# Attention and feed-forward block on one core: shift rows issued from ScalarE's queue, the mean of y folded into constants, x normalised in one operation, second query copy ahead of the squares

## The reference

```python
x = x + xattn(layernorm(x), ctx)      # 16 heads, scores of 64 x 64, softmax over the context
x = x + ffn(layernorm(x), w1, w2)     # 256 -> 1024 -> 256

kv_rope = kv_c * cos + rotate_half(kv_c) * sin
scores  = q_r @ k_r.T                  # q_r from Wq, w_kc_q, W_qr; k_r from kv_rope, W_kr
attn    = softmax(scores)
out     = ((attn @ kv_rope) @ w_kc_kv.T) @ Wo.T

def bitlinear158(x, w):
    xn = x / norm(x) * sqrt(d)
    xq = clip(round(xn * s), -128, 127) / s       # s = 127 / max|xn| of the row
    wq = clip(round(w / mean|w|), -1, 1) * mean|w|
    return xq @ wq.T
ffn = bitlinear158(gelu(bitlinear158(x, w1)), w2)
```

## Time and profile before

| | us |
|---|---|
| median of 3 runs | 534.22 |
| the runs | 529.8, 535.0, 534.22 |
| the profiled execution | 530.62, span 528.8 |
| PE busy | 424.0 (80%) |
| DVE busy | 404.1 (76%) |
| ACT busy | 256.1 (48%) |
| POOL busy | 233.6 (44%) |

### The profile page before, as it was taken

One profiled execution on the slowest core, in us unless ns is written; L12 is line 12 of the kernel. 1 busy time (PEld: TensorE's weight loads), 2 busy tenths in 40 slices (PEclk: granted clock), 3 DMA queues, 4 the chain that ended last, 5 costly groups with the idle time before them and its releaser, 6 DMA issues.

```text
span 528.8 us, 9004 instructions
## 1 busy us (share of the span) xinstructions
PE 424.0 (80%) x2823; PEld 298.8 (57%) x2823; DVE 404.1 (76%) x926; ACT 256.1 (48%) x464; POOL 233.6 (44%) x301
## 2 busy tenths in 40 slices
PE   3998787978678788989798989798889877585664
PEld 1488654656546565757485748475647553353432
DVE  0545147888879987989899897988887989886794
ACT  0111263523255646565567474756564747355430
POOL 0300502445334546465555555554645464646432
PEclk9999999999799988999999989998989999987865
DMA  8990901111132303344425253433534344335243
GB/s 237 349 296 1 355 4 43 43 41 43 42 57 61 77 13 93 60 109 74 93 65 104 60 98 62 94 72 81 82 72 76 78 82 73 82 71 114 65 100 80
DMA packets 62800, 48.96 MB, mean 93 GB/s; under 512 B 51169, under 2 KB 56289, under 8 KB 61729
## 3 DMA queue, kind: packets, MB, share of 16 engines
q1 hardware_dynamic: 62752, 48.39, 38.5%
HBM read 32.11 MB, written 4.46 MB: 69 GB/s over the span
## 4 chain that ended last, share of the span: by engine, by line
DVE 30%; DMA 16%; PE 15%; issue 15%; SPq 10%; ACT 3%; POOL 0%; DVEq 0%; ACTq 0%; POOLq 0%
DMA rb<-rinv_d 9%; DMA rinv_d<-ri 5%; DVE cr L841 5%; SPq L422 4%; DVE fw L197 3%; DVE red L811 3%; PE ps L736 3%; DMA shift<-nmax 2%; DVE fw L196 2%; SPq L430 2%; DVE fw L194 2%; DVE red L818 2%; SPq L436 2%; DVE amax L866 2%; DVE ri L834 2%
## 5 line engine op out<-in xcount | busy, mean ns | idle before, releaser
L482 POOL TENSOR_TENSOR cl<-cr,ch 128x512 fp32r<-128x512 f32 x64 | 80.2, 1275 | 178.7 <-ACT ch L563 178.7
L563 ACT ACTIVATE ch<-cr 128x512 fp32r<-128x512 f32 x64 | 39.3, 632 | 100.2 <-DVE cr L841 100.2
L712 PE MATMUL hps<-bh,ch 128*128 128x256 f32 x256 | 78.3, 306 | 8.2 <-issue 8.0
L663 PE MATMUL ps<-xh,ah 128*128 128x256 f32 x256 | 77.5, 303 | 1.7 <-DVE xl L803 1.4
L714 PE MATMUL hps<-bh,cl 128*128 128x256 f32 x256 | 73.8, 288 | 0.0
L713 PE MATMUL hps<-bl,ch 128*128 128x256 f32 x256 | 73.7, 288 | 0.0
L664 PE MATMUL ps<-xl,ah 128*128 128x256 f32 x256 | 72.7, 284 | 0.0
L665 PE MATMUL ps<-xh,al 128*128 128x256 f32 x256 | 72.6, 283 | 0.0
L545 ACT ACTIVATE qf<-ps 128x512 f32<-128x512 f32 x64 | 37.5, 587 | 65.3 <-PE ps L665 65.3
L663 PEld LDWEIGHTS ps<-xh,ah 128*128 128x128 f32 x256 | 49.9, 195 | 19.8 <-issue 16.2
L712 PEld LDWEIGHTS hps<-bh,ch 128*128 128x128 f32 x256 | 51.1, 199 | 11.5 <-issue 11.5
(11 more groups left out here) (116 smaller groups left out, 925.7 us busy)
## 6 DMA issues: line engine op xcount, KB each, us to landing
rb<-rinv_d SPq DMA_DIRECT2D x64, 256.0 KB, 3.9
xs<-x SPq DMA_DIRECT2D x4, 1024.0 KB, 23.1
out<-yo SPq DMA_DIRECT2D x32, 128.0 KB, 2.0
wq_s<-wq SPq DMA_DIRECT2D x1, 2048.0 KB, 20.1
wo_s<-wo_t SPq DMA_DIRECT2D x1, 2048.0 KB, 9.2
w_s<-w_t SPq DMA_DIRECT2D x2, 1024.0 KB, 12.5
rinv_d<-ri SPq DMA_DIRECT2D x128, 2.0 KB, 1.4
wk_a<-wk_t SPq DMA_DIRECT2D x2, 512.0 KB, 6.1
```

The costliest lines, as they stand in the source:

```text
L482: pool.tensor_tensor(cl[:, u % 2, :, b * S:(b + 1) * S], cr[:, :, b * S:(b + 1) * S], ch[:, u % 2, :, b * S:(b + 1) * S].bitcast(F32), ALU ...
L663: pe.matmul(o, ah[:, c, cols], xh[:, k % 2, c, :], start=(c == 0), stop=False)
L712: pe.matmul(O[:, 0:D], c_h, bh[:, hp, :], start=(hp == 0), stop=False)
```

## The change

- `shift_rows` moves from SP's list to ACT's. It stands there behind the first query copy (and `x_hi`) and ahead of `ctx_hi`.
- The mean of y is no longer made on its own. `centre` computes -256 x + sum instead of x - mean, in one operation as before; constants (`least`, `FLOOR1`, the sign of `level`) take up the factor.
- `norm_x` is one operation per tile: x * rstd - mean * rstd, where `nmean` now holds the product.
- The second query copy of a step, `q_out(k, b + 1)`, stands ahead of the squares instead of behind them.
- In PE's list the first `up` of an odd step stands ahead of the shifts instead of behind them.

```diff
@@ -216,10 +214,10 @@
             c = slice(half * NT // 2, (half + 1) * NT // 2)
             n = half * (RSQRT_OPS + 2) + 1
             dve.wait_ge(sem["bn_means"], (half + 1) * NT // 2)
-            dve.tensor_scalar(nmean[:, c], mv[:, c, 0], -1.0, None, ALU.mult).then_inc(sem["rstd_steps"], 1)
             dve.tensor_scalar(nw[0][:, c], mv[:, c, 1], EPS_LN, None, ALU.add).then_inc(sem["rstd_steps"], 1)
-            dve.wait_ge(sem["rstd_steps"], n + 1)
-            rsqrt(dve, nw[0][:, c], rstd[:, c], nw[1][:, c], sem["rstd_steps"], n + 1)
+            dve.wait_ge(sem["rstd_steps"], n)
+            rsqrt(dve, nw[0][:, c], rstd[:, c], nw[1][:, c], sem["rstd_steps"], n)
+            dve.scalar_tensor_tensor(out=nmean[:, c], in0=mv[:, c, 0], scalar=-1.0, in1=rstd[:, c], op0=ALU.mult, op1=ALU.mult).then_inc(sem["rstd_steps"], 1)
 
         cos_t = cst[:, 0:DC]
         em_c = cst[:, 2 * DC:2 * DC + 2 * P]
@@ -258,8 +256,9 @@
             def _(pool):
                 pool.memset(ones[:, :], 1.0).then_inc(sem["const_set"], 1)
                 for k, w in ((0, D), (1, F)):
-                    pool.memset(least[:, 2 * k:2 * k + 2], EPS_N ** 2 * (EPS_LN if k == 0 else 1.0) / w).then_inc(sem["eps_set"], 1)
-                pool.memset(level[:, :], 1.0 / 127.0).then_inc(sem["eps_set"], 1)
+                    pool.memset(least[:, 2 * k:2 * k + 2], EPS_N ** 2 * (EPS_LN * D ** 2 if k == 0 else 1.0) / w).then_inc(sem["eps_set"], 1)
+                pool.memset(level[:, 0:2], -1.0 / 127.0).then_inc(sem["eps_set"], 1)
+                pool.memset(level[:, 2:4], 1.0 / 127.0).then_inc(sem["eps_set"], 1)
                 pool.wait_ge(sem["consts_loaded"], 16)
                 pool.wait_ge(sem["kv_loaded"], 16)
                 pool.tensor_tensor(rot[:, :, hd:DC], kv_s[:, :, 0:hd], wide(cst[:, DC + hd:2 * DC]), ALU.mult).then_inc(sem["rope_steps"], 1)
...
@@ -405,14 +404,6 @@
         with nc.Block() as block:
             @block.sync
             def _(sp):
-                def shift_rows(u):
-                    p = u % 2
-                    sp.wait_ge(sem["row_maxima"], u + 1)
-                    at_least(sp, sem["shifted"], 2 * (u - 1))
-                    for gg in range(2):
-                        sp.dma_start(shift[BB * gg:BB * gg + 2, p, :].bitcast(F32).rearrange("b (k s) -> b k s", s=32),
-                                     nmax[:, p, 32 * gg:32 * gg + 32].bitcast(F32)).then_inc(sem[f"shift_rows{p}"], 16)
-
                 def rinv_rows(u):
                     p = u % 2
                     sp.wait_ge(sem["rinv_steps"], 2 * u + 2)
@@ -457,8 +448,6 @@
                         turn_g(n - 10)
                     if tile(n - 12):
                         store(n - 12)
-                    if tile(n):
-                        shift_rows(n)
                     if tile(n - 1):
                         rinv_rows(n - 1)
                         rinv_spread(n - 1)
@@ -469,12 +458,9 @@
             def _(pool):
                 def norm_x(t):
                     at_least(pool, sem["xt_made"], t // 2)
-                    at_least(pool, sem["x_normed"], 2 * t)
                     if t == NT // 2:
                         pool.wait_ge(sem["rstd_steps"], 2 * (RSQRT_OPS + 2))
-                    pool.tensor_scalar(xc[:, :], xs[:, t, :], 1.0, nmean[:, t:t + 1], ALU.mult, ALU.add).then_inc(sem["x_normed"], 1)
-                    pool.wait_ge(sem["x_normed"], 2 * t + 1)
-                    pool.tensor_scalar(xn[:, t % 2, :], xc[:, :], rstd[:, t:t + 1], 0.0, ALU.mult, ALU.add).then_inc(sem["x_normed"], 1)
+                    pool.tensor_scalar(xn[:, t % 2, :], xs[:, t, :], rstd[:, t:t + 1], nmean[:, t:t + 1], ALU.mult, ALU.add).then_inc(sem["x_normed"], 1)
 
                 def ctx_lo(u, b):
                     pool.wait_ge(sem["ctx_hi"], 2 * u + b + 1)
@@ -483,11 +469,11 @@
                 def centre(t):
-                    pool.wait_ge(sem["means"], t + 1)
+                    pool.wait_ge(sem["residuals"], t + 1)
                     at_least(pool, sem["x_squared"], t - YR + 1)
                     at_least(pool, sem["x_maxima"], t - YR + 1)
                     at_least(pool, sem["x_scaled"], t - YR + 1)
-                    pool.tensor_scalar(yc[:, t % YR, :], xs[:, t, :], 1.0, mean2[:, t:t + 1], ALU.mult, ALU.add).then_inc(sem["x_centred"], 1)
+                    pool.tensor_scalar(yc[:, t % YR, :], xs[:, t, :], -float(D), xsum[:, t:t + 1], ALU.mult, ALU.add).then_inc(sem["x_centred"], 1)
 
                 def x_round(t):
                     pool.wait_ge(sem["x_scale_steps"], 2 * (t // 2 + 1))
@@ -595,6 +581,14 @@
                     act.wait_ge(sem["b_made"], q + 1)
                     act.activation(bh[:, 2 * q:2 * q + 2, :], FOLD[q].rearrange("p (h d) -> p h d", d=D), ACT.Copy).then_inc(sem["b_hi_done"], 1)
 
+                def shift_rows(u):
+                    p = u % 2
+                    act.wait_ge(sem["row_maxima"], u + 1)
+                    at_least(act, sem["shifted"], 2 * (u - 1))
+                    for gg in range(2):
+                        act.dma_start(shift[BB * gg:BB * gg + 2, p, :].bitcast(F32).rearrange("b (k s) -> b k s", s=32),
+                                     nmax[:, p, 32 * gg:32 * gg + 32].bitcast(F32)).then_inc(sem[f"shift_rows{p}"], 16)
+
                 x_hi(0)
                 for b in range(4):
                     q_out(0, b)
@@ -611,17 +605,19 @@
                         q_out(k, b)
                     if n % 2 and k + 1 < NB:
                         x_hi(k + 1)
+                    if tile(n):
+                        shift_rows(n)
                     if n == 0:
                         w_sum(1)
                     if tile(n - 2):
                         ctx_hi(n - 2, 0)
                         ctx_hi(n - 2, 1)
+                    if k < NB:
+                        q_out(k, b + 1)
                     if tile(n - 4):
                         square_x(n - 4)
                     if tile(n - 8):
                         square_g(n - 8)
-                    if k < NB:
-                        q_out(k, b + 1)
                     if tile(n):
                         exp(n, 0)
                         exp(n, 1)
@@ -639,7 +635,7 @@
             @block.tensor
             def _(pe):
                 def x_t(k):
-                    pe.wait_ge(sem["x_normed"], 4 * k + 4)
+                    pe.wait_ge(sem["x_normed"], 2 * k + 2)
                     free_bank(pe, "x", k)
                     for c in range(KC):
                         for t in range(2):
@@ -779,12 +775,13 @@
                         pe.matmul(O[:, 0:2], ones[:, :], wabs[:, :], start=True, stop=True).then_inc(sem["w_totals"], 1)
                     if k < NB:
                         queries(k, b + 1)
+                    if n % 2 and tile(n - 7):
+                        up(n - 7, 0)
                     if tile(n):
                         shifts(n)
                     if turns(n):
                         kv_t((n + 2) // 4)
                     if n % 2 and tile(n - 7):
-                        up(n - 7, 0)
                         up(n - 7, 1)
                     if tile(n - 1):
                         if n == 1:
@@ -843,11 +840,8 @@
 
                 def residual(t):
                     dve.wait_ge(sem["projected"], t + 1)
-                    at_least(dve, sem["means"], t - 1)
                     dve.scalar_tensor_tensor(out=xs[:, t, :], in0=O[:, 0:D], scalar=1.0, in1=xs[:, t, :], op0=ALU.mult, op1=ALU.add,
-                                             accum_out=xsum[:, t % 2:t % 2 + 1]).then_inc(sem["residuals"], 1)
-                    dve.wait_ge(sem["residuals"], t + 1)
-                    dve.scalar_tensor_tensor(out=mean2[:, t:t + 1], in0=xsum[:, t % 2:t % 2 + 1], scalar=-1.0 / D, in1=ones[:, 0:1], op0=ALU.mult, op1=ALU.mult).then_inc(sem["means"], 1)
+                                             accum_out=xsum[:, t:t + 1]).then_inc(sem["residuals"], 1)
 
                 def x_max(t):
                     dve.wait_ge(sem["x_centred"], t + 1)
@@ -857,7 +851,7 @@
 
                     c = slice(2 * p, 2 * p + 2)
                     dve.wait_ge(sem["x_maxima"], 2 * p + 2)
-                    dve.scalar_tensor_tensor(out=gm[:, c], in0=amax[:, p, 0:2], scalar=FLOOR1, in1=level[:, :], op0=ALU.max, op1=ALU.mult).then_inc(sem["x_scale_steps"], 1)
+                    dve.scalar_tensor_tensor(out=gm[:, c], in0=amax[:, p, 0:2], scalar=FLOOR1, in1=level[:, 0:2], op0=ALU.max, op1=ALU.mult).then_inc(sem["x_scale_steps"], 1)
                     dve.wait_ge(sem["x_scale_steps"], 2 * p + 1)
                     dve.reciprocal(c1[:, c], gm[:, c]).then_inc(sem["x_scale_steps"], 1)
 
...
```

More of the change, by code:

```diff
@@ L85, in build @@
         nmean = sb("nmean", [P, NT], F32)
-        mean2 = sb("mean2", [P, NT], F32)
+        xsum = sb("xsum", [P, NT], F32)
         c1 = sb("c1", [P, NT], F32)
@@ L92, in build @@
         least, wfactor = [sb(n, [P, 4], F32) for n in ("least", "wfactor")]
```

(10 more changed lines are left out.)

## The result

The changed kernel takes **535.63 us** in the median of 20 runs (532.06 to 539.78); the kernel before, run beside it, 532.66 us (20 runs, 525.99 to 535.0). The ratio is 1.0074, 95% interval 1.0049 to 1.0098: slower by 0.7%, less than the 1% that the prediction calls no change. Every ratio here compares only the runs within 1.5% of their kernel's fastest, so it can differ from that of the medians by up to about 1%. Forecast: 537. The profiled execution took 532.06 (span 530.3), against 530.62 (span 528.8) before.

A forecast was written before the change was run, and what follows sets the result against it. ACT, then DVE, bounds both gaps; start +1.4, early loop -3.5, tiles 8 to 10 +1.8, ten pairs of gaps, gap 30 to 31 +0.84 and end -2.0 sum to +4.7 us: forecast 537 us, range 518 to 551.

The forecast's parts named there:

- The bound: Gaps between row maxima: even 10.66 us and odd 14.80 us, both bound by ACT, then DVE.
- The eye-catching 40.1 us: PE's total idle ahead of the shifts; if PE decided, the kernel would reach 510 us, chance 0.10.
- Issues on ACT: Two shift issues ahead of ctx_hi take 1.38 us; ctx_hi at +1.74, even gaps 11.50 us instead of 10.66.
- The neighbouring bounds of 0.85 and 2.48 us: Two issues' length on ACT: cheap at 0.85 gives 525 us, chance 0.13; dear at 2.48 gives 561, chance 0.13.
- The norms: Odd gaps: norms start at +5.3 and take 5.0 us, 4.38 to the maxima; 14.7 us against 14.92.
- the lock in the Trainium skill: DVE and POOL share a port pair exclusively: norms fall to 4.3 us, total 530; chance of freed norms 0.08.
- The start: Before tile 1: 1.1 us gained by single normalising, second weight sum 2.5 us later on ACT; net +1.4 us.
- The early loop: Divisions of tiles 2, 3 and 5 wait less for `rb` through the folded mean: -3.5 us.
- my bounds of 0 and 6: Limits on the gain at the divisions of tiles 2, 3 and 5: 0 to 6.0 us, the sum of their waits.
- The end: Behind tile 31: -1.0 us for earlier norms, -1.0 for SP's queue and the last means; -2.0 us.
- The sum: All terms over the whole kernel: +4.7 us, giving 535.3 by the profiled time or 538.9 by the median's.
- the division's 1.09 us wait: Odd divisions wait 1.09 us for `rb`; folding the mean shortens that loop by 1.06 us and removes the wait.

The follow-up runs named there:

- the small operation back: Changed kernel plus one small DVE operation per tile where the mean stood, POOL waiting for it: 536.53 us, 1.0137 to the kernel before.
- the move alone: Kernel before with only the two shift issues moved to ACT's list: 537.01 us, 1.0083 to the kernel before.
- the kernel with the sum first: Changed kernel with the second sum of weights ahead of the first shift issue on ACT: 531.0 us, 1.0044 to the kernel before.
- the best kernel here: Changed kernel with shift issues on SP, second query copy behind the squares, and store behind the shift rows: 506.52 us (506.96 with store ahead).

## Why the prediction was right, and where its terms were off

**The bound.** Right. ACT's ctx_hi, squares and exp, then DVE's unbroken work, set both gaps. Four kernels show it apart: one, two and three issues move ctx_hi and the even gap alike, and moving the store shortens PE's wait for no gain. The eye-catching 40.1 us moved to `up` and to DVE.

**Issues on ACT.** I took 1.38 us from SP's row; they take 1.27, and ctx_hi stands at +1.68, not +1.74. Even gap 11.36 for 11.50 foretold, with DVE's wait for exp at 2.78 for 2.9 and the wait for the squares at 2.45 for 2.4; one odd gap of ten fell under 14 (13.89, tile 29). The neighbouring bounds of 0.85 and 2.48 us were both wrong rows to hold to: the first were issues of 2 KB, the second transposes.

**The norms.** Foretold start +5.3 and length 5.0: in the mean of the odd gaps +5.16 and 4.70 (before 5.08 and 5.14), counted to the start of the partial sums as in the prediction. This pair, with 4.5 us from there to the maxima, is why odd gaps came out at 14.35 and not 14.7: 3.8 us over ten gaps, the largest error in the sum. An L195 still lasts 1.06 us (336.22 to 337.28). In the profile of the change POOL rounds from 336.17 to 337.28 there. By the lock in the Trainium skill (page "SBUF — State Buffer", section "SBUF: two separate sides") I had worked out 4.3. This row agrees with holding DVE to POOL's end, yet putting the second POOL operation of each tile back (0.41 us, two of them under the norms of an odd gap) lengthened the norms by 0.04 to 0.11 us, not by 0.8, so the operation's length is not the price. Half of the 0.44 us that the norms lost hangs on the place of the query copy: with the copy late they take 4.92. The rule fits single instructions, also one with a single input (an L191 of tile 27 takes 1.08 us from 411.86, while POOL rounds from 411.80 to 412.91; in tile 21 it takes 0.17); that the number of instructions that meet a POOL operation sets the price is my reading, not tested.

**The start.** +2.5 foretold between tiles 0 and 1, +4.40 measured, the term furthest off for its size. Timelines of the changed kernel, ACT, DVE and PE, answering to the earlier trace rows:

```profile
70.04 1.89 ACTq L589 DMA_DIRECT2D shift<-nmax  x2
72.03 1.91 ACT L577 ACTIVATE pe<-w_s 128x2048 f32<-128x2048 f32 x1 [2.98 <-issue]
...
69.73 0.28 DVE L821 TENSOR_REDUCE nmax<-hps 32x64 fp32r<-32x128 f32 x1 [1.55 <-PE hps L685]
...
74.09 0.40 PE L775 MATMUL hps<-wabs,ones 128*128 128x2 f32 x2 [3.38 <-ACT pe L577]
```

Windows of the same (busy time of each engine with its count, then the granted clock of PE, DMA share, GB/s):

```profile
70.00:74.00 4.00, 0.71 (x8) 0.18 (x4) 0.01 (x1) 1.97 (x2) 0.00 (x0) 1.00 0.01 2
74.00:77.06 3.06, 2.97 (x15) 2.97 (x15) 0.76 (x5) 0.04 (x1) 0.00 (x0) 0.55 0.00 0
77.06:83.00 5.94, 4.81 (x34) 2.89 (x35) 3.95 (x7) 3.64 (x7) 0.87 (x2) 0.94 0.00 0
```

Two things were not in the sum. The first two issues take 1.89 us, not 1.27. And PE, idle for 3.38 us, comes back at a granted clock of 0.55 (near its lower level of 1.2 GHz, half of 2.4): the 12 products of queries start 0.21 us apart instead of 0.12, about 1.1 us. How long the lower level lasts behind the same pause is not the same in every profile: with `up` back behind the shifts, PE also idles 3.38 us there, its clock is 0.51 over the next 3.40 us and 0.50 over the 3.60 behind them, and the step takes 16.04 us, 2.4 more than in the change. With the sum ahead of the issues PE waits 0.29 us, the queries run at a granted 1.00, and the long issues delay nothing. Timeline of that kernel, PE:

```profile
71.68 0.38 PE L775 MATMUL hps<-wabs,ones 128*128 128x2 f32 x2 [0.29 <-ACT pe L577]
```

**The early loop.** -3.5 foretold for the mean, -4.57 with one even gap's loss of 0.7 in it, so about -5.3: inside my bounds of 0 and 6. But not all of it is the mean's. With the small operation back these tiles take 90.93 us instead of 88.90, so 2.0 are (the operation still takes up to 1.07 us in the first tiles); the move alone gave 1.1 (92.41 for 93.47). The rest is not taken apart, and like kernels differ by over 1 us here (89.20 and 87.98 with the shift on SP and the copy late).

**The end.** -2.0 foretold, +0.21 measured. The 1.0 us behind tile 31's squares came: its projections start 11.22 us after the maxima instead of 12.22. Then PE spent it. The projections of the change:

```profile
467.42:472.00 4.58, 4.58 (x29) 4.45 (x33) 2.63 (x5) 2.49 (x5) 1.89 (x2) 0.69 0.02 5
```

and of the kernel before:

```profile
467.13:470.40 3.27, 3.27 (x29) 3.14 (x33) 2.60 (x5) 2.12 (x5) 0.57 (x1) 1.00 0.63 107
```

The same 29 products take 1.3 us longer at a granted clock of 0.69, behind idle times of PE of 1.69 and 2.43 us; before they ran at 1.00 behind busy time, since the pause of that kernel (4.83 us ahead of tile 31's shift) lay earlier. Two of my terms (start and end) thus ended in the clock that PE gets behind a pause, which I had priced at nothing. That this cost is the clock's is read from rows; no kernel was made to test it, but the profiles differ in it by themselves: from the start of these projections to the contexts behind them, with the same work behind like pauses, the change takes 4.38 us at 0.68, the kernel with the sum first 5.35 at 0.53, and the one with the small operation back 5.60 at 0.50. What these pauses cost thus differs from profile to profile.

**The sum** was +4.7, the two profiles give +1.5, and the ratio is 0.74% (+2.6 to +5.2 us by its interval). By the profiles it landed near through errors that partly cancel: odd gaps 3.8, early loop 2.0 and even gaps 1.5 us too dear, start 1.6 and end 2.2 too cheap. That it came within 2 us of the median is in part luck. The step that failed in mechanism is the mean. I took its 1.06 us for its length in every order of the work, and gave the end of the division's 1.09 us wait to folding it. But it is that long only while POOL's `ctx_lo` begins ahead of it, and moving the shift rows puts ctx_hi, and POOL behind it, 0.78 us later: then the mean takes 0.16 us even unfolded, and the division's wait goes too (the move alone, above). So the folded mean is worth 20 us as long as the shift rows stay on SP, and almost nothing once they have moved. Both parts remove the same lateness of SP's list, and I had priced no version with one of them and not the other.

**Open:** how much of the norms' 0.44 us is POOL's shorter list (0.04 to 0.11 by putting it back into the change; 0.27 between the kernel with only the shift moved, 5.19, and the change with the copy late, 4.92, which differ in more than this list); whether a mean of 1.06 us would cost time with the shift on ACT.

## What to carry to other kernels

Before moving a transfer's issue to a computing engine's queue, look at what stands behind it on that engine and whether that is on the chain: two issues of 0.63 us cost 18 us here, while the 40 us of waits that they removed were worth nothing. Follow the gaps between equal instructions on the engine that ends them, not totals of waits. Two edits that relieve the same queue don't add up, so time each alone and without the other: the best kernel here (507 us) keeps one and drops the other. And don't take an instruction's length from one order over into another: look at what the neighbouring engine runs at that moment in the new order.
